# Carried strips contiguous in both buffers: 32 rows of 2 KB for each DMA

## The reference

```python
q = (h @ Wq).reshape(S, 16, 64)          # h: normed x, 512 x 128; k and v likewise
scores = einsum('qhd,khd->hqk', q, k) / sqrt(64) + position_bias
probs = softmax(scores, axis=-1)
ctx = einsum('hqk,khd->qhd', probs, v).reshape(S, 1024)
out = ctx @ Wo
```

## Time and profile before

| | |
|---|---|
| time, median of 3 runs | 1776.68 us (1772.99 to 1780.63) |
| the profiled execution | 1773.84 us, span 1772.1 us, mean granted TensorE clock 0.927 |
| attention b | about 630 to 1650 us of the span |
| busy in the whole span | PE 77%, ACT 52%, DVE 50%, POOL 15% |
| DMA packets | 233,384, of which 211,981 under 2 KB; 161.21 MB |

### The profile page before, as it was taken

The page is one execution under the profiler, slowest core; times in us unless marked ns, Lnnn a source line. Parts: engine busy times, 40 slices in busy tenths (PEclk is TensorE's granted clock), DMA queues, the critical chain, the costliest instruction groups (busy, mean ns, idle before and its releaser), DMA issues. The chain is left out here.

```text
span 1772.1 us, 22492 instructions
## 1 busy us (share of the span) xinstructions
PE 1371.6 (77%) x6711; PEld 604.9 (34%) x6711; DVE 880.3 (50%) x2700; ACT 930.0 (52%) x1844; POOL 269.2 (15%) x277
## 2 busy tenths in 40 slices
PE   2488888886638189898899898898898997996364
PEld 1123223221226033343343343343433433432253
DVE  2445554543311056567557467467467466575211
ACT  0377766666413066656556566456465565564031
POOL 4101112221224300000100100101002002001235
PEclk9999999999859589999999999899999999999677
DMA  3355444457047224434335344344344244344052
GB/s 67 78 106 137 105 103 95 91 107 133 13 129 238 32 53 89 92 77 106 88 81 106 86 88 102 82 88 101 77 87 104 62 96 90 67 100 95 21 143 24
DMA packets 233384, 161.21 MB, mean 91 GB/s; under 512 B 36414, under 2 KB 211981, under 8 KB 233264
## 3 DMA queue, kind: packets, MB, share of 16 engines
q1 hardware_dynamic: 222256, 153.39, 39.4%
q0 software_dynamic: 11008, 6.39, 2.6%
HBM read 61.75 MB, written 36.09 MB: 55 GB/s over the span
## 5 line engine op out<-in xcount | busy, mean ns | idle before, releaser
L1473 DVE CUSTOM_DVE_ANT_0 tile<-s_ps,bias 128x512 f32<-128x512 f32 x512 | 331.2, 684 | 204.0 <-issue 147.7
L1401 ACT ACTIVATE tile<-tile,low 128x512 f32<-128x512 f32 x512 | 363.0, 715 | 3.2 <-DVE low L1473 3.2
L628 ACT ACTIVATE probs_a<-score_ps,gbound 128x1024 f32<-128x1024 f32 x256 | 268.8, 1114 | 151.7 <-PE score_ps L857 125.4
L1283 PE MATMUL s_ps<-kT,qT 64*128 64x512 f32 x1024 | 266.4, 640 | 57.6 <-ACT kT L1385 57.6
L1393 ACT ACTIVATE pT<-p_ps 128x512 f32<-128x512 f32 x256 | 152.7, 597 | 295.7 <-PE p_ps L1291 265.1
L1306 PE MATMUL o_psb<-pT,v_b 128*64 128x512 f32 x512 | 238.6, 610 | 16.0 <-DMA crossed<-blocks 14.6
L1306 PE MATMUL o_psb<-crossed,v_b 128*64 128x512 f32 x512 | 238.9, 610 | 0.0
L857 PE MATMUL score_ps<-q_stack,k_stack 128*128 128x512 bf16 x512 | 146.1, 396 | 45.8 <-DMA q_stack<-q_parts 21.2
L1484 DVE STREAM_TRANSPOSE blocks<-tile 128x512 f32<-128x512 f32 x256 | 180.9, 706 | 0.3 <-issue 0.3
L1291 PE MATMUL p_ps<-ident,tile 128*128 128x128 f32 x1024 | 166.2, 285 | 16.1 <-ACT pT L1393 11.0
L1291 PEld LDWEIGHTS p_ps<-ident,tile 128*128 128x128 f32 x1024 | 108.8, 142 | 203.4 <-issue 156.9
(11 more groups left out here) (152 smaller groups left out, 1443.2 us busy)
## 6 DMA issues: line engine op xcount, KB each, us to landing
crossed<-blocks SPq DMA_DIRECT2D x1024, 64.0 KB, 2.1
inv_row<-inv_rows SPq DMA_DIRECT2D x128, 128.0 KB, 2.9
k_stack<-k_parts SPq DMA_DIRECT2D x96, 96.0 KB
q_stack<-q_parts SPq DMA_DIRECT2D x96, 96.0 KB
bias_skew<-bias_rows SPq DMA_DIRECT2D x8, 1024.0 KB
w_f<-in_w SPq DMA_DIRECT2D x32, 256.0 KB, 5.3
bias<-bias_skew SPq DMA_DIRECT2D x16, 448.0 KB
q_parts<-parts SPq DMA_DIRECT2D x40, 128.0 KB, 2.4
```

What stands on the lines that cost most here:

```text
L628: nc.scalar.activation(probs[q % 2][:, c % 4, :], score_ps[c % 2][:, :], ACT.Exp, bias=gbound[:, :]).then_inc(p_ready.sem, 1)
L1283: last = nc.tensor.matmul(s_ps[k % 2][s][:, :], qT[n % 2][own(s), i * P:(i + 1) * P], kT[n % 2][own(s), :], start=True, stop=True)
L1401: nc.scalar.activation(tile[k % RING][s][:, :], tile[k % RING][s][:, :], ACT.Exp, bias=low[n % 2][:, s, i:i + 1], scale=-1.0, accum_out=su ...
L1473: nc.vector.tensor_tensor_reduce(out=tile[k % RING][s][:, :], in0=s_ps[k % 2][s][:, :], in1=bias[:, h, off:off + S], scale=1.0, scalar=3.0e38,
```

## The change

`blocks` was laid out [128, 16, 4, 32]: column block c*4 + m, query tile i, 32 queries. It becomes [128, m, c, i, 32], so that all that goes to the destination group m lies together, 512 floats for each partition. `crossed` was [128, c, a, i, 32] and becomes [128, a, c, i, 32], so that all that comes from source group a lies together. A DMA of `cross` so moves 32 rows of 2 KB, contiguous on either side; before, each row was four pieces of 512 B, 2 KB apart. The transpose of VectorE writes, and the matmul of TensorE reads, through the new steps. Number, order and bytes of the DMAs, all waits and all of the schedule stay; the projections stay in the odd double steps.

```diff
-        NB = S // BLK
+        STRIPS = P // BLK
...
-        blocks = [sb(f"blocks{n}", [P, NB, TB, BLK]) for n in two]
-        crossed = [sb(f"crossed{n}", [P, TB, P // BLK, TB, BLK]) for n in two]
+        blocks = [sb(f"blocks{n}", [P, STRIPS, TB, TB, BLK]) for n in two]
+        crossed = [sb(f"crossed{n}", [P, STRIPS, TB, TB, BLK]) for n in two]
...
-        CROSS = 16 * TB * (P // BLK)
+        CROSS = 16 * STRIPS * STRIPS
...
-                src = blocks[n % 2][:, :, :, :].rearrange("p (c m) i j -> p c m (i j)", m=P // BLK)
-                dst = crossed[n % 2][:, :, :, :, :].rearrange("p c a i j -> p c a (i j)")
-                for a in range(P // BLK):
-                    for m in range(P // BLK):
-                        sp.dma_start(dst[m * BLK:(m + 1) * BLK, :, a, :],
-                                     src[a * BLK:(a + 1) * BLK, :, m, :]).then_inc(crossed_in[n % 2], 16)
+                for a in range(STRIPS):
+                    for m in range(STRIPS):
+                        sp.dma_start(crossed[n % 2][m * BLK:(m + 1) * BLK, a, :, :, :].rearrange("p c i j -> p (c i j)"),
+                                     blocks[n % 2][a * BLK:(a + 1) * BLK, m, :, :, :].rearrange("p c i j -> p (c i j)")
+                                     ).then_inc(crossed_in[n % 2], 16)
...
-                             crossed[n % 2][:, kt, :, :, :].rearrange("p a i j -> p i a j"))
+                             crossed[n % 2][:, :, kt, :, :].rearrange("p a i j -> p i a j"))
...
-                nc.vector.transpose(blocks[n % 2][:, :, i, :], tile[k % RING][1][:, :]).then_inc(blocked.sem, 1)
+                nc.vector.transpose(blocks[n % 2][:, :, :, i, :].rearrange("p m c j -> p c m j"), tile[k % RING][1][:, :]).then_inc(blocked.sem, 1)
```

## The result

After takes 1771.72 us (median of 20 runs, 1764.81 to 1777.61) against 1776.52 for before in the same series (20 runs, 1772.75 to 1781.45). The ratio is 0.9974, 95% interval 0.9962 to 0.9987: 4.8 us less, where 13.3 were forecast. The profiled execution of after has a span of 1769.9 us; that of before has 1772.1.

What follows compares the result with a forecast made beforehand. TensorE sets the pace and waits for strips that SyncE's queue issues late. First pair 2.7, middle 2.9, last pair 6.0 and clock 1.7 make 13.3 us less: 1763.4 us against the median 1776.68 (-0.75%), range 1757 to 1778.

Steps and rivals of the forecast that it cites:

- What bounds the kernel: Second attention: TensorE sets the pace; its value matmuls wait 14.6 us in 7 places for strips because SyncE's queue is late.
- Part 1, the issue: A crossing's DMA on SyncE costs 0.43 us instead of 601 ns, so the sixteenth issue starts 2.55 us earlier.
- A: Rival: issue cost unchanged at 0.59 to 0.60 us, set by kind of transfer; about 1 us gained, 1775.7 us; chance 0.30.
- Part 1, transport: Crossing's DMAs on the engines: 0.30 us in 512 B packets become 0.18 in 2 KB ones, landing 0.12 us earlier.
- First pair: TensorE's 3.03 us wait for the strips before the first pair's value matmuls shrinks by 2.7 us.
- Middle: The five waits for strips between first and last pair, none over 1.09 us, go whole: 2.9 us.
- Last pair: SyncE, late twice before the last crossing, gains 3.3 us ahead of it and 2.7 in it: 6.0 us.
- The clock: Slow stretch of value matmuls at granted clock 0.68 behind the first wait goes: 1.7 us gained.
- Parts 2 and 3: New steps in VectorE's transpose writes and in TensorE's matmul reads of crossed cost nothing: 0 for each.
- B: Rival: issue cost in between, 0.50 us; 8.5 us gained, 1768.2 us; chance 0.12.
- D: Rival: issue as cheap as k_stack's, pitch 0.41 us; 16.3 us gained, 1760.4 us; chance 0.52 together with the forecast.
- C: Rival: VectorE's transposes pay for the new steps, +66 us at the upper bound, about 1829 us; chance 0.06.

Runs made afterwards that it cites:

- e3: After with a seventeenth DMA, 32 rows of 2 KB from blocks to DRAM, ahead of each crossing's sixteen: 1778.13 us, ratio 1.0021 to before.
- e4: Half of the change: blocks laid out as in after, crossed as in before, so each DMA writes four pieces: 1775.06 us, ratio 1.0001 to before.
- e2: After without the four DMAs of a crossing whose source and destination group are the same, a quarter not carried: 1757.53 us, ratio 0.9914 to before.
- e1: Separate kernel that computes nothing: SyncE issues 14 kinds of DMA, six back to back; all nine kinds from SBUF to SBUF cost 589 to 606 ns.
- clean series: The last series of runs, with before and after each profiled again without edits; before takes 1710.01 us (18 runs), the scatter stalls nobody.
- e5: Before run again without an edit, for a second profile: 1775.85 us.
- e8: After with the router's scatter in attention b left out, so layer four's experts read blank slots: 1712.91 us in one run.
- e6: After run again without an edit, for a second profile: 1784.47 us.
- e11: Before run without an edit in the last series, for a third profile: 1709.46 us in one run.
- e12: After run without an edit in the last series, for a third profile: 1703.40 us in one run.
- e7: After with the four diagonal strips of each crossing copied by GpSimd instead of by DMA, all work kept: 1757.24 us, ratio 0.9884 to before.
- e10: After with the diagonal strips copied by GpSimd instead of by DMA, timed again in the last series: 1703.9 us, ratio 0.9967 to before.

## Why the prediction came out as it did

**What bounds the kernel** was right, SyncE's queue. It is late at the first pair, at the last, and at some places between, and the size of the effect follows the landing: as in before or a little later (e3), 1.0021; as in before (e4), 1.0001; 0.34 us earlier (after), 0.9974; about 2.9 us earlier (e2), 0.9914. Packets and read patterns have no part in it that shows: e3 has after's and none of its gain. One reading was wrong: the wait of 0.9 us that the earlier trace rows puts down to ScalarE's pT was to stay. It is pair 33's, at 1175.52 us, where the last strip had landed at 1175.38; in after it is gone, so it was a wait for the strips.

**Part 1, the issue: the step that failed.** "I take 0.43 us ... the new DMA is nearest to w_raw and k_stack in shape." It was nearest in the shape of its rows, and inside SBUF the price does not go by that: e1 shows 590 ns from SBUF to SBUF for the same rows that cost 421 from DRAM and 424 to it. The pitch went from 0.649 (9.734/15) to 0.631 us (9.459/15), so the sixteenth issue starts 0.28 us earlier, not 2.55.

The rows of before could not decide it. The only ones from SBUF to SBUF were the crossings, at 601, and both cheap rows had DRAM on one side, so none priced the new DMA. I sorted them by pieces, and that fitted all but inv_row, which I explained away; sorted by DRAM, q_parts would not have fitted either. The open question was worth more than the 0.30 that A got.

**Part 1, transport.** 0.12 us was forecast; the time to landing went from 2.10 to 2.04 us. It was mis-sized by half. The share of the queue in the whole span fell from 39.4% to 36.2%, by which, with the prediction's 38 ns for a packet of 512 B, one of 2 KB comes to some 124 ns (an estimate), not 90: 8 x 38 = 0.30 us become 2 x 124 = 0.25. The 90 was read from packets behind inv_row, which come from DRAM. The Trainium skill, "DMA: Bandwidth & Descriptors", section Why small descriptors are slow (HBM only), says that copies inside SBUF don't suffer from small descriptors. The trace agrees nearly: the crossings land 0.06 us earlier with 98,304 packets fewer, and e1's landing from start is 2.0 us for whole rows and 2.0 for pieces.

**What it takes off the path**, term by term, from the clean series's pair of profiles:

- First pair: 2.7 forecast, 0.2 measured (31.5 to 31.3 us).
- Middle: 2.9 forecast as the whole of the waits. There 3.5 us went (3.3 in the mean of the three pairs of profiles) although the landing moved by 0.34 only. They did not go whole: before waits 4.3 us there in this series and after 1.2. That 3.5 comes near 2.9 is partly luck: there was more to lose than the forecast counted, and not all of it went. What holds, and would have held under rival A too, is that such waits are short and a little takes away most of them.
- Last pair: 6.0 forecast, 0.65 measured, in two steps of 0.33 and 0.32. The structure was right (SyncE late twice); each time the queue gained its 0.3 us, and no more.
- The clock: 1.7 forecast, nothing that the change brought. In after the stretch behind the first wait is as in the earlier trace rows, 5.28 us at a granted clock of 0.68 for sixteen matmuls, a part of them at the 1.2 GHz level:

```profile
658.27:663.55 5.28, 5.28 (x16) 1.74 (x16) 0.00 (x0) 0.17 (x2) 0.00 (x0) 0.68 0.38 104
```

  But the loss is not in every execution of before. In e5, the same kernel with the same wait of 3.03 us, the 5.28 us behind it stand at 1.00 and hold 24 matmuls:

```profile
654.70:659.98 5.28, 5.28 (x24) 1.92 (x24) 1.07 (x2) 0.00 (x0) 0.00 (x0) 1.00 0.43 100
```

  The step from the first pair's value matmuls to the second's shows it: 15.5 us in before, after, e4 and e8, 13.8 in e5, e6, e11, e12 and e3, all behind waits of 2.7 to 3.1 us. So the prediction counted as a property of the kernel what one profile happened to have; in the clean series neither kernel has it. In the ten us from the first scores on, the four slow ones have a granted clock of 0.76 to 0.85, the five others of 0.70 to 0.71. e2 and e7 have 0.84 and 0.86 there and wait only 0.17 and 0.30 us: their step takes 13.8. What decides between the two is open.
- Sum: 0.2 + 3.5 + 0.65 = 4.4 us, against the 4.8 between the medians of the result. The tails (130.7 and 128.2) run the same code and lie within the 127.5 to 130.7 of all profiles with their scatter, so they aren't counted.

The same account fits e2, whose landing moved about as far as the forecast's. Its profile against that of before: first values 3.6 us earlier, clock 1.7, the 54 middle steps 4.5, the last two 4.8, in all 14.6 where the forecast had 13.3. The last pair was put too high (6.0), the first (2.7) and the middle (2.9) too low, and only their sum was close.

**Parts 2 and 3** were right at 0: the transpose and the matmul kept 707 and 611 ns, and e4 carries the new write for nothing.

**The rivals.** A was right in its issue price, and inside SBUF in the reason that it gave ("the cost belongs to the kind of transfer, not to its pieces"); what makes up the kind, e1 leaves open. Its own sum, 1 us, was too small, because it gave each wait 0.12 us where the landing moved by 0.34: it left out that even a small difference of the issue, 0.02 us in the mean, is paid fifteen times. B and D fell with the 591 ns in after, C with the transposes.

## What to carry to other kernels

A DMA's issue can't be priced from rows of another kind of transfer: where no row goes from the same memory to the same memory, a small kernel that only issues DMAs (e1) gives the price, and a row that doesn't fit should not be explained away. Where a queue issues many DMAs for one wait, dropping a DMA is worth far more than reshaping it (four fewer: 0.9914; all sixteen reshaped: 0.9974), but what takes over the work must not run beside a chain that feeds the critical engine. And a change of 5 us is not to be read from one profile of each kernel, nor is a clock that fell in one profile a property of the kernel: cut the spans at marks, see which stretches vary with unchanged code, and compare step by step.

## What the runs showed of the hardware

- SyncE's issue (e1): 589 to 606 ns from SBUF to SBUF, from 32 rows of 128 B to 128 rows of 2 KB; 424 ns to DRAM with 32 rows of 2 KB, but 607 for q_parts; 421 and 432 ns from DRAM with 32 and 128 rows, but 596 ns with 64, repeated or not.
- In the two series with before at 1774 to 1778 us, router steps with the scatter's eight indirect DMAs took 5 to 8 us more than without it (e8); in the series with before at 1710 us they took none more, with the same program.
- Behind a wait of 2.7 to 3.1 us the granted clock fell (0.68 over the next 5.28 us in after) in four executions and stayed at 1.00 in five, before and after alike in both groups.
- Two small VectorE operations beside GpSimd's copies took 0.57 and 0.64 us instead of 0.19, while the 128x512 transposes kept their mean of 706 ns (e10).
